# The shared expert of the last expert stage, moved from the main loop into the time of the router

## The reference

```python
scores = sigmoid(h @ gate_w.T)                       # 32 experts
sc = scores + gate_bias
group_scores = top_k(sc.reshape(-1, 8, 4), 2)[0].sum(-1)
gmask = best 4 of the 8 groups
tki = top_k(where(gmask, sc, 0), 8)[1]
tkw = 2.5 * scores[tki] / sum(scores[tki])
g, u = silu(h @ w_gate[e].T), h @ w_up[e].T          # 64 wide, e = 0..31
routed = sum over e of (g * u * combine[:, e]) @ w_down[e].T
shared = silu(h @ sh_gate.T) * (h @ sh_up.T) @ sh_down.T
return routed + shared
```

## Time and profile before

| | |
|---|---|
| median of three runs | 3116.63 us (3113.25 to 3116.71) |
| the profiled execution: its own time | 3116.61 us |
| its span from the first to the last instruction | 3114.8 us |
| PE busy | 2705.1 us, 87% of the span |
| DVE busy | 2057.1 us, 66% |
| ACT busy | 1571.8 us, 50% |
| POOL busy | 1074.1 us, 34% |
| mean granted TensorE clock | 0.935 of full speed |

### The profile page before, as it was taken

The page is one execution under the profiler, slowest core; times in us unless marked ns, Lnnn a source line. Parts: engine busy times, 40 slices in busy tenths (PEclk is TensorE's granted clock), DMA queues, the critical chain, the costliest instruction groups (busy, mean ns, idle before and its releaser), DMA issues. The chain is left out here.

```text
span 3114.8 us, 55189 instructions
## 1 busy us (share of the span) xinstructions
PE 2705.1 (87%) x21256; PEld 1691.7 (54%) x21276; DVE 2057.1 (66%) x4308; ACT 1571.8 (50%) x3080; POOL 1074.1 (34%) x784
## 2 busy tenths in 40 slices
PE   8995899989899799998999798798877899777698
PEld 5552455567676566665567566465643334335465
DVE  5758999945644665647554665466548999996554
ACT  4334688862423444444544555365457676643122
POOL 3201000001143344434443444154227777773000
PEclk9995899989899899999999899998999999998899
DMA  1000000001120200000000000000013344340000
GB/s 55 1 4 1 2 3 3 3 2 61 49 92 22 84 1 1 1 1 1 1 1 1 29 1 1 1 1 1 1 52 135 136 143 143 137 141 27 1 1 14
DMA packets 34228, 105.41 MB, mean 34 GB/s; under 512 B 3456, under 2 KB 14592, under 8 KB 33200
## 3 DMA queue, kind: packets, MB, share of 16 engines
q1 hardware_dynamic: 31952, 97.69, 9.0%
q0 software_dynamic: 2016, 4.19, 0.4%
HBM read 94.01 MB, written 7.86 MB: 33 GB/s over the span
## 5 line engine op out<-in xcount | busy, mean ns | idle before, releaser
L2082 POOL TENSOR_TENSOR many_probs<-many_probs,many_rinv 128x2048 f32<-128x2048 f32 (+7 forms) x128 | 269.8, 2107 | 371.6 <-DVE many_rinv L2121 371.6
L1062 DVE TENSOR_REDUCE heads_halfmax<-heads_qmajor 128x1 f32<-128x512 f32 x512 | 316.4, 681 | 32.8 <-PE heads_qmajor L923 29.4
L3477 DVE TENSOR_TENSOR_SCAN stream_state<-stream_decay,stream_state 128x512 f32<-128x512 f32 x256 | 306.3, 1233 | 0.8 <-ACT stream_decay L3309 0.5
L1027 ACT ACTIVATE weights<-heads_kmajor 128x1024 f32<-128x1024 f32 x256 | 259.3, 1027 | 71.7 <-PE heads_kmajor L935 66.3
L2051 ACT ACTIVATE many_probs<-many_score,many_negmax 128x1024 f32<-128x1024 f32 (+7 forms) x256 | 187.4, 737 | 179.7 <-DVE many_negmax L2105 175.9
L2105 DVE TENSOR_REDUCE many_negmax<-many_score 128x1 f32<-128x1024 f32 (+7 forms) x256 | 184.4, 751 | 110.4 <-PE many_score L1980 108.9
L3147 PE MATMUL stream_yacc<-stream_state,ident 128*128 128x512 f32 x512 | 249.1, 614 | 0.4 <-POOL stream_state L3439 0.4
L3309 ACT ACTIVATE stream_decay<-weights,mamba_negA 128x512 f32<-128x512 f32 x256 | 173.0, 689 | 112.5 <-DVE stream_state L3477 111.3
L3439 POOL TENSOR_TENSOR stream_state<-XN,stream_state 128x1024 f32<-128x1024 f32 x85 | 200.4, 2360 | 81.4 <-DVE stream_state L3477 81.1
L1988 PE MATMUL many_ring<-ident,many_probs 128*128 128x128 f32 x1152 | 177.4, 282 | 28.1 <-POOL many_probs L2082 6.5
L3468 DVE TENSOR_TENSOR stream_state<-stream_bspread,stream_du 128x1024 f32<-128x1024 f32 x128 | 153.2, 1197 | 46.5 <-POOL stream_du L3415 38.6
(11 more groups left out here) (585 smaller groups left out, 6023.7 us busy)
## 6 DMA issues: line engine op xcount, KB each, us to landing
XN<-mamba_crows SPq DMA_DIRECT2D x85, 512.0 KB, 3.6
stream_crow<-mamba_crows SPq DMA_DIRECT2D x43, 512.0 KB, 3.6
weights<-in_w_dram SPq DMA_DIRECT2D x1, 6148.0 KB, 17.8
weights<-in_w_dram SPq DMA_DIRECT2D x1, 4274.0 KB, 12.8
weights<-in_w_dram SPq DMA_DIRECT2D x1, 3296.0 KB, 10.7
swiglu_pairs<-swiglu_fetched SPq DMA_DIRECT2D x1, 2310.0 KB, 10.2
weights<-in_w_dram SPq DMA_DIRECT2D x1, 2112.0 KB, 7.9
swiglu_fetched<-swiglu_pairs SPq DMA_DIRECT2D x4, 528.0 KB, 7.3
```

Source lines behind the costliest of these rows:

```text
L1027: nc.scalar.activation(probs_of(k).rearrange("p (a n) -> p a n", a=2), kmajor[:, at:at + 2, :], ACT.Exp, scale=SC).then_inc(exp_done, 1)
L1062: nc.vector.tensor_reduce(halfmax[:, g % 2, at, h % 2:h % 2 + 1], qmajor[:, (2 * n + j) % 3, :], AX, ALU.max).then_inc(max_done, 1)
L2082: nc.gpsimd.tensor_tensor(pair, pair, rinv[:, n % 4, :].unsqueeze(2).broadcast_to([P, 2, wide]), ALU.mult).then_inc(norm_done, 1)
L3477: nc.vector.tensor_tensor_scan(h[:, part(half)], decay[:, (2 * g + half) % DECAYS, :], h[:, part(half)], 0.0 if half == 0 else h[:, BANK - ...
```

## The change

The shared expert leaves the main loop. `UNITS` has 4 x 16 = 64 units. PE computes the shared expert's gate and up products for each of the four `tc` (`shared_up`) and its down products (`shared_down`) right after the router product, before the `gate_and_up` of units 0 and 1, while DVE runs the router chain. ACT makes the silu and also copies the up product out of PSUM, POOL multiplies the two in SBUF (it cannot read PSUM), and ACT copies the result of the down product into `m.Y`. In the main loop DVE adds `down` to `m.Y` after the sixteenth unit of a `tc`, where it copied after the seventeenth. `wide_ones`, its memset and its product are gone. `shared` is double-buffered and holds silu, up product and their product side by side. The new semaphores are counted up by: `sh_up` PE, `sh_silu`, `sh_kept` and `sh_y` ACT, `sh_hid` POOL, `sh_down` PE, `bias_kept` DVE. The diff, with the list of semaphore names cut:

```diff
--- before.py
+++ after.py
@@ -3537,7 +3537,7 @@
 
     w = weight_views(m, s)
     E, G, PERG, CH = 32, 8, 4, 16
-    UNITS = [(tc, c) for tc in range(NT // 4) for c in range(CH + 1)]
+    UNITS = [(tc, c) for tc in range(NT // 4) for c in range(CH)]
     with Phase(nc, "grouped") as ph:
         scores = ph.sb("scores", [P, NT, E])
         biased = ph.sb("biased", [P, NT, E])
@@ -3555,33 +3555,38 @@
         partsT = ph.sb("partsT", [96, TOKENS], BF16)
         select = ph.sb("select", [96, CH, P], BF16)
         silu = ph.sb("silu", [P, 2, BANK])
-        wide_ones = ph.sb("wide_ones", [1, BANK])
+        shared = ph.sb("shared", [P, 2, 3, BANK])
         gated = ph.sb("gated", [P, 2, BANK])
         hidden = ph.sb("hidden", [P, 3, BANK])
         gate_up = ph.ps("gate_up", 4)
         spread = ph.ps("spread", 2)
         down = ph.ps("down", 1)
         turned = ph.ctx.enter_context(nc.psum_tensor("grouped_turned", [P, 1, 1024], BF16))
...
         nz = Normaliser(nc, m, ph, "n_", True, False, EARLY[s])
         block = ph.block()
         shared_w = (w["sg"], w["su"], w["sd"])
 
         @block.gpsimd
         def _(pool):
-            nc.gpsimd.memset(wide_ones[:], 1.0).then_inc(sel_done, 1)
             nc.gpsimd.memset(select[:], 0.0).then_inc(sel_done, 1)
             for r in range(3):
-                pool.wait_ge(sel_done, r + 2)
+                pool.wait_ge(sel_done, r + 1)
 
                 nc.gpsimd.affine_select(out=select[:].rearrange("k c (j i) -> k c j i", j=2),
                                         in_=select[:].rearrange("k c (j i) -> k c j i", j=2),
                                         compare_op=ALU.not_equal, fill=1.0, base=-E * r,
                                         pattern=[[-2, CH], [-1, 2], [0, 64]], channel_multiplier=1).then_inc(sel_done, 1)
+            for tc in range(NT // 4):
+                pool.wait_ge(sh_silu, tc + 1)
+                pool.wait_ge(sh_kept, tc + 1)
+                nc.gpsimd.tensor_tensor(shared[:, tc % 2, 2, :], shared[:, tc % 2, 0, :], shared[:, tc % 2, 1, :],
+                                        ALU.mult).then_inc(sh_hid, 1)
             for q in EARLY[s]:
                 nz.root(pool, 0, q)
 
@@ -3599,9 +3604,37 @@
                 if n >= 2:
                     pe.wait_ge(gated_done, n - 1)
                 for k in range(2):
-                    wt = shared_w[k] if c == CH else w[("wg", "wu")[k]][:, c * P:(c + 1) * P]
+                    wt = w[("wg", "wu")[k]][:, c * P:(c + 1) * P]
                     nc.tensor.matmul(gate_up[:, 2 * (n % 2) + k, :], wt, m.HT[:, tc * BANK:(tc + 1) * BANK],
                                      start=True, stop=True).then_inc(gu_done, 1)
+            def shared_up(tc):
+                if tc >= 2:
+                    pe.wait_ge(sh_silu, tc - 1)
+                    pe.wait_ge(sh_kept, tc - 1)
+                for k in range(2):
+                    last = nc.tensor.matmul(gate_up[:, 2 * (tc % 2) + k, :], shared_w[k],
+                                            m.HT[:, tc * BANK:(tc + 1) * BANK], start=True, stop=True)
+                last.then_inc(sh_up, 1)
+
+            def shared_down(tc):
+                pe.wait_ge(sh_hid, tc + 1)
+                if tc == 0:
+                    pe.wait_ge(bias_kept, 1)
+                if tc >= 1:
+                    pe.wait_ge(sh_y, tc)
+                for j in range(4):
+                    last = nc.tensor.matmul(down[:, 0, j * P:(j + 1) * P], shared[:, tc % 2, 2, j * P:(j + 1) * P],
+                                            shared_w[2], start=True, stop=True)
+                last.then_inc(sh_down, 1)
+            shared_up(0)
+            shared_up(1)
+            for tc in range(NT // 4):
+                shared_down(tc)
+                if tc + 2 < NT // 4:
+                    shared_up(tc + 2)
+            pe.wait_ge(sh_y, NT // 4)
+            pe.wait_ge(sh_kept, NT // 4)
+            pe.wait_ge(sh_silu, NT // 4)
             gate_and_up(0)
             gate_and_up(1)
             pe.wait_ge(parts_done, 1)
@@ -3614,34 +3647,42 @@
                                                parts[:, g, :, :].rearrange("p r e -> p (r e)"), m.identb[:])
                 last.then_inc(turn_done, 1)
             pe.wait_ge(turn_kept, 2)
-            pe.wait_ge(sel_done, 5)
+            pe.wait_ge(sel_done, 4)
             for n in range(len(UNITS) + 1):
                 if n < len(UNITS):
                     tc, c = UNITS[n]
                     if n >= 2:
                         gate_and_up(n)
                         pe.wait_ge(hid_done, n - 1)
-                    if c < CH:
-                        nc.tensor.matmul(spread[:, n % 2, :], select[:, c, :], partsT[:, tc * BANK:(tc + 1) * BANK],
-                                         start=True, stop=True).then_inc(spread_done, 1)
-                    else:
-                        nc.tensor.matmul(spread[:, n % 2, :], m.ones[0:1, :], wide_ones[0:1, :], start=True,
-                                         stop=True).then_inc(spread_done, 1)
+                    nc.tensor.matmul(spread[:, n % 2, :], select[:, c, :], partsT[:, tc * BANK:(tc + 1) * BANK],
+                                     start=True, stop=True).then_inc(spread_done, 1)
                 if n >= 1:
                     tc, c = UNITS[n - 1]
                     pe.wait_ge(hid_done, n)
                     if c == 0 and tc > 0:
                         pe.wait_ge(y_done, tc)
                     for j in range(4):
-                        wt = shared_w[2] if c == CH else w["wd"][:, c * P:(c + 1) * P]
+                        wt = w["wd"][:, c * P:(c + 1) * P]
                         last = nc.tensor.matmul(down[:, 0, j * P:(j + 1) * P], hidden[:, (n - 1) % 3, j * P:(j + 1) * P],
-                                                wt, start=(c == 0 and j == 0), stop=(c == CH), skip_group_check=True)
+                                                wt, start=(c == 0 and j == 0), stop=(c == CH - 1), skip_group_check=True)
                     last.then_inc(down_done, 1)
 
         @block.scalar
         def _(act):
             act.wait_ge(router_done, 1)
             nc.scalar.activation(scores[:].rearrange("p t e -> p (t e)"), spread[:, 0, :], ACT.Sigmoid).then_inc(sig_done, 1)
+            for tc in range(NT // 4 + 1):
+                if tc < NT // 4:
+                    act.wait_ge(sh_up, tc + 1)
+                    if tc >= 2:
+                        act.wait_ge(sh_hid, tc - 1)
+                    nc.scalar.activation(shared[:, tc % 2, 0, :], gate_up[:, 2 * (tc % 2), :], ACT.Silu).then_inc(sh_silu, 1)
+                    nc.scalar.activation(shared[:, tc % 2, 1, :], gate_up[:, 2 * (tc % 2) + 1, :],
+                                         ACT.Copy).then_inc(sh_kept, 1)
+                if tc >= 1:
+                    act.wait_ge(sh_down, tc)
+                    nc.scalar.activation(m.Y[:, 4 * tc - 4:4 * tc, :].rearrange("p t n -> p (t n)"), down[:, 0, :],
+                                         ACT.Copy).then_inc(sh_y, 1)
             for half in range(2):
                 act.wait_ge(turn_done, half + 1)
                 nc.scalar.activation(partsT[:, half * 1024:(half + 1) * 1024], turned[0:96, 0, :],
@@ -3661,7 +3702,8 @@
             def tt(out, a, b, op):
                 chain.step(nc.vector.tensor_tensor(out, a, b, op))
             dve.wait_ge(bias_done, 1)
-            chain.step(nc.vector.tensor_copy(biasB[:], down[:, 0, 0:E]))
+            nc.vector.tensor_copy(biasB[:], down[:, 0, 0:E]).then_inc(bias_kept, 1)
+            dve.wait_ge(bias_kept, 1)
             dve.wait_ge(sig_done, 1)
             tt(biased[:], scores[:], biasB[:].unsqueeze(1).broadcast_to([P, NT, E]), ALU.add)
             a, b, c, d = (biased[:].rearrange("p t (g k) -> p t g k", k=PERG)[:, :, :, k] for k in range(PERG))
@@ -3719,11 +3761,12 @@
                         dve.wait_ge(down_done, n - 2)
                     nc.vector.tensor_tensor(hidden[:, n % 3, :], spread[:, n % 2, :], gated[:, n % 2, :],
                                             ALU.mult).then_inc(hid_done, 1)
-                if n >= 1 and UNITS[n - 1][1] == CH:
+                if n >= 1 and UNITS[n - 1][1] == CH - 1:
                     tc = UNITS[n - 1][0]
                     dve.wait_ge(down_done, n)
-                    nc.vector.tensor_copy(m.Y[:, 4 * tc:4 * tc + 4, :].rearrange("p t n -> p (t n)"),
-                                          down[:, 0, :]).then_inc(y_done, 1)
+                    dve.wait_ge(sh_y, tc + 1)
+                    y = m.Y[:, 4 * tc:4 * tc + 4, :].rearrange("p t n -> p (t n)")
+                    nc.vector.tensor_tensor(y, down[:, 0, :], y, ALU.add).then_inc(y_done, 1)
                 if n < len(UNITS) and UNITS[n][0] >= 1:
                     tc, c = UNITS[n]
                     if c == 2:
```

(9 more changed lines are left out.)

## The result

The changed kernel took 3099.24 us, the median of six runs (3097.91 to 3102.25), where the kernel before took 3113.03 us (3110.42 to 3116.71): ratio 0.9958, 95% interval 0.9946 to 0.9969. The profiled execution took 3097.91 us, its span 3096.1 us, its mean granted clock 0.937. A second series gave 3102.43 against 3112.52 us, 0.9967 (0.9955 to 0.9979). The forecast of 3104.0 us is 4.8 us above the measured median, and 3.6 us of that is the kernel before, which took 3113.03 us over six runs where the forecast started from 3116.63.

What follows compares the result with a forecast made beforehand. PE was taken to set the loop's pace, DVE's chain the end of the gap ahead of it. Terms -14.40 - 0.32 - 1.29 - 0.25 + 3.6 + 0.1 = -12.6 took 3116.6 to 3104.0 us, range 3098.5 to 3107.5.

Steps and rivals of the forecast that it cites:

- The loop: Main loop, 68 to 64 units: 60 periods of 2.83 us where 184.20 us were before, -14.40 us.
- its end: Last unit: hidden 2.71 us after its gate product instead of 3.03, without the row of ones, -0.32 us.
- PE's new work hidden: Gap ahead of the loop: some 12 us of shared products fit in PE's idle time before DVE's chain ends, 0 us.
- GpSimd's products: Router chain: POOL's products hold up DVE's two-input instructions, three of four counted, +3.6 us (bounds 0 and +5.1).
- The lost memset: Before the router chain: POOL's 0.52 us memset goes, affine_select ends earlier and DVE gains, -0.25 us (0 to -0.52).
- The table load: After the last partsT: the 1.28 us silu table load moves behind the sigmoid, first silu starts earlier, -1.29 us.
- TensorE's clock: Start of the loop: same half-clock start after about 9 idle microseconds of PE, 0 us (bounds 1.8 either way).
- Semaphore clearing: End of the stage: one more instruction, 0 to +0.2 us, taken as +0.1.
- Rival A: Router chain: POOL's products cost DVE next to nothing, one stall or none; 3100.4 to 3101.7 us, chance 0.18.
- rival B: Loop start: at full clock since PE worked in the gap, 1.8 us less, 3102.2 us; chance 0.08.
- C: Gap ahead of the loop: shared work runs at half clock, PE ends 3 us behind DVE's chain; 3107 us, chance 0.11.
- D: Gap ahead of the loop: shared slices strictly one after another at half clock, 17.3 us behind the chain; 3121 us, chance 0.02.

Runs made afterwards that it cites:

- the kernel with bf16 ones: Kernel before, its shared-expert product of ones on bf16 instead of float32 operands; first gate pass to last write of Y 225.80 us, against 228.15.
- the early-table run: Kernel before plus one unused single-column silu right behind the sigmoid; first gate pass to last write of Y 227.47 us, against 228.15.
- the held back products: Changed kernel, GpSimd's products waiting for steps 10 and 22 of DVE's chain; first gate pass to last write of Y 212.98 us, against 215.80.

## Why the prediction was right, point by point

The forecast was 12.6 us less; the stretch gave 12.35, and the medians 13.8 and 10.1. That the stretch came within 0.3 us is in part luck, as the last paragraph of this section shows.

- **The loop** (-14.40) and **its end** (-0.32): -14.40 and -0.31, unit by unit as counted. The addition into `Y` cost nothing, as said.
- **PE's new work hidden**: right. The forecast had units 0 and 1 done 19.6 us after the first gate pass (2896.7 - 2877.1); they were (2890.38 - 2870.77), and the instructions on the way stood within 0.3 us of their forecast places. The cover was 8.8 us, forecast 9.
- **GpSimd's products**: mechanism and count right, three stalls and the third product free. The size was off: +3.6 forecast, +2.85 measured by leaving the products out. The three longer instructions give the same sum (1.00, 0.96 and 0.88 where I had put 1.27, 1.27 and 1.1). The timeline shows why: the stopped instruction starts 0.1 to 0.25 us after the product of 1264 ns and ends some 0.2 us after the product, so it is not longer by the whole product.
- **The lost memset** (-0.25): the addition of the bias took 0.69 where it took 0.93: -0.24. With one memset more (the kernel with bf16 ones) it took 1.14, so it does follow the end of GpSimd's work. In the chain as a whole 0.12 us was left of it (25.67 before, 25.55 without products), so in the chain the term is half the size forecast.
- **The table load** (-1.29): -1.41 at the first down product. The load itself is 1.28 of it, so the further drain of 1.38 us that the prediction set aside does not show (with it the sum would have been 3102.6 and not 3102.7).
- **TensorE's clock** (0): the step that failed. I took the same half-clock start to begin earlier and end earlier with it. The start was at half clock, as said, but the early-table run showed that its end stayed where it was, which alone makes +0.68. In the changed kernel the rise came 0.7 us later after the turning as well, and the term measured +1.04, inside the bounds of 1.8.
- **Semaphore clearing** (+0.1): 0.

The errors of single terms are larger than that of the sum: the chain came out 0.62 us under its forecast (GpSimd's products 0.75 under, the memset 0.13 over), the table load 0.12 under, the clock 1.04 over. Together they make 0.3, since those of the products and of the clock nearly cancelled, and that was luck. Rival A (products free) is refuted by the run without them, rival B (full clock at the start) by the 0.50 in the window above. The conditions of C and D were not met here: the down products between the shared gate products took 1.05 to 1.16 us, the full-clock time, and units 0 and 1 took 3.70. C's appeared once the products were held back.

## What to carry to other kernels

Work moved from the queue of the bounding engine into that engine's idle time is worth its full time, and it can be counted from two starts in the timeline; then check what it runs beside. Here a product of 1.26 us on "idle" GpSimd cost DVE's chain 0.9 to 1.0 us wherever DVE read two SBUF operands, and nothing beside maxima, searches or match steps: place it there, or do it on DVE from PSUM for about the same price (here 2.34 us for four, against 2.85). When an edit makes PE start earlier after a wait, look at when its clock rises: a gain ahead of the rise counted half or less here (0.74 of 1.42 us, and 0.37 of 1.41), and a wait inserted on PE cost 2.2 us through the clock where the wait itself would have been hidden.

## What the runs showed of the hardware

The Trainium skill (SBUF — State Buffer, "Who interferes with whom") calls the shared port pair an exclusive lock; the runs agree for two-input DVE work, 1250 against 294 ns, and show none of it on one-input MAX8 and match steps (176 and 174 ns beside the held back products, 176 and 175 in the kernel before). Nine unread float32 products in PE's idle time made the stretch 1.9 us shorter, with three more in the short waits 3.6. With twenty ahead of the turning and none in the short waits the clock fell to 0.50 behind the second wait of 1.11 us. And the start of this last stage scattered over 8.7 us between profiles of programs that are the same up to there; most of the difference of the first two (5.7 of 6.3 us) arose between 690 and 790 us, and why was not tried.
